# Mamba mixer in a vision tower: GpSimd makes the scan input of 4 of 16 units in SBUF, and the softplus scratch moves into an output buffer

## What is computed

```python
xz = einsum('bld,ed->ble', xn, in_proj_w)            # 512 -> 2 x 1024
x_inner, z = split(xz, 2)
xc = silu(causal_conv4(x_inner) + conv_b)            # 1024 channels
x_ssm = einsum('bld,ed->ble', xc, x_proj_w)          # 33 rows: B (16), C (16), one step
dt = softplus(x_ssm[..., -1:] * dt_w[:, 0] + dt_b)
A = -exp(A_log)                                      # 1024 x 16
def step(h, (dt_t, B_t, C_t, u_t)):
    h = exp(dt_t[..., None] * A) * h + (dt_t * u_t)[..., None] * B_t[:, None, :]
    y_t = sum(h * C_t[:, None, :], axis=-1) + D_param * u_t
return einsum('ble,de->bld', y * silu(z), out_proj_w) + residual
```

## Time and profile before

| what | value |
|---|---|
| median of 3 runs | 3200.05 us (3198.8 to 3203.89) |
| the profiled execution, its own time | 3196.83 us |
| its span in the profile | 3195.2 us |
| busy, whole span | PE 2581.1 us, DVE 1982.7, ACT 1351.8, POOL 1149.4 |
| mixer, first to last of its parts | about 455 us to 1721 us of the span |

### The profile page before, as it was taken

The page is one execution under the profiler, slowest core; times in us unless marked ns, Lnnn a source line. Parts: engine busy times, 40 slices in busy tenths (PEclk is TensorE's granted clock), DMA queues, the critical chain, the costliest instruction groups (busy, mean ns, idle before and its releaser), DMA issues. The chain is left out here.

```text
span 3195.2 us, 47773 instructions
## 1 busy us (share of the span) xinstructions
PE 2581.1 (81%) x17110; PEld 2128.3 (67%) x17111; DVE 1982.7 (62%) x2707; ACT 1351.8 (42%) x3260; POOL 1149.4 (36%) x694
## 2 busy tenths in 40 slices
PE   5999986778888888888877603999994699999997
PEld 5999986777788878788766501444442466666665
DVE  7557336999999999999995520222222655655453
ACT  1332527777777777777772200111110122222222
POOL 3000004666666666666662054010012422222110
PEclk9989978899988999999998756999997788988897
DMA  5600001000000000000000054555555110110000
GB/s 216 275 1 1 1 1 48 34 28 29 28 29 28 29 29 28 29 28 28 28 28 7 0 179 123 184 178 189 167 168 154 55 28 29 29 29 28 8 8 14
DMA packets 63510, 201.48 MB, mean 63 GB/s; under 512 B 12347, under 2 KB 17595, under 8 KB 60475
## 3 DMA queue, kind: packets, MB, share of 16 engines
q1 hardware_dynamic: 25210, 96.31, 8.9%
q0 software_dynamic: 26272, 80.77, 7.9%
q10 hardware_dynamic: 11808, 21.50, 1.8%
HBM read 130.31 MB, written 68.23 MB: 62 GB/s over the span
## 5 line engine op out<-in xcount | busy, mean ns | idle before, releaser
L832 POOL TENSOR_TENSOR m_hs<-m_hs,m_BC 128x1040 f32<-128x1040 f32 x256 | 617.0, 2410 | 333.5 <-DVE m_hs L940 333.5
L752 ACT ACTIVATE m_dA<-m_dt,m_A 128x128 f32<-128x128 f32 x2048 | 616.3, 388 | 268.6 <-DVE m_hs L940 149.6
L631 PE MATMUL m_py<-m_hs,ident 128*128 128x130 f32 x4096 | 568.1, 297 | 166.8 <-POOL m_hs L832 166.6
L631 PEld LDWEIGHTS m_py<-m_hs,ident 128*128 128x128 f32 x4096 | 534.4, 210 | 186.2 <-POOL m_hs L832 183.8
L940 DVE TENSOR_TENSOR_SCAN m_hs<-m_dA,m_own 128x1040 f32<-128x1040 f32 x256 | 593.4, 2318 | 21.6 <-DVE m_own L929 15.9
L929 DVE TENSOR_TENSOR m_own<-m_BC,m_own 128x1040 f32<-128x1040 f32 x256 | 317.7, 1241 | 11.4 <-DVE m_hs L940 3.6
L583 PE MATMUL m_pw<-m_xg,m_w_in 128*128 128x130 f32 x2048 | 259.4, 285 | 47.3 <-DVE m_xc L893 36.2
L583 PEld LDWEIGHTS m_pw<-m_xg,m_w_in 128*128 128x128 f32 x2048 | 249.1, 199 | 53.1 <-DVE m_xc L893 41.7
L1335 PE MATMUL e_pG<-e_w_gu,e_xT 128*128 x656 | 235.5, 503 | 11.0 <-issue 8.3
L1315 POOL DMA_DIRECT2D e_x<-slots x80 | 43.0, 538 | 403.8 <-PE e_pX L1326 396.9
L1335 PEld LDWEIGHTS e_pG<-e_w_gu,e_xT 128*128 128x128 f32 x656 | 119.8, 192 | 91.6 <-issue 25.4
(11 more groups left out here) (263 smaller groups left out, 4630.9 us busy)
## 6 DMA issues: line engine op xcount, KB each, us to landing
m_BC<-xs SPq DMA_DIRECT2D x16, 2080.0 KB, 8.7
slots<-a_zero POOLq DMA_DIRECT2D x48, 512.0 KB, 39.0
e_w_gu<-in_gate_up_w SPq DMA_DIRECT2D x32, 768.0 KB
e_x<-slots POOLq DMA_DIRECT2D x82, 256.0 KB
slots<-e_y ACTq DMA_DIRECT2D x82, 256.0 KB, 2.2
e_w_d<-in_down_w SPq DMA_DIRECT2D x32, 256.0 KB
out_h<-t_ho SPq DMA_DIRECT2D x8, 520.0 KB, 3.3
a_AT<-in_A_cols SPq DMA_DIRECT2D x8, 512.0 KB, 7.3
```

Source lines behind the costliest of these rows:

```text
L631: mm = pe.matmul(py[k % 2][:, 0:MT], ident[:, :], hs[u % NB][:, n, :], start=False, stop=(half == 1 and n == HN - 1))
L752: act.activation(images(dA[u % NB][:, n, :])[:, :, 1:TOK], images(dt[b][:, k, :])[:, :, 1:TOK], ACT.Exp, scale=A[:, at:at + 1]).then_inc(d ...
L832: pool.tensor_tensor(hs[u % NB][:, :, :], hs[u % NB][:, :, :], BC[b][:, ST + half * HN:ST + (half + 1) * HN, :], ALU.mult).then_inc(prod_r ...
```

## The change

POOL makes the scan's input of units 3, 7, 11 and 15 of every step, in a new SBUF tile `pool_bu`, out of three instructions; it does so behind its products of units 0, 4, 8 and 13. DVE's scan of those four units reads `pool_bu` in SBUF instead of `own` in PSUM, and DVE makes the input of the other twelve. DVE still makes `du` of all eight tiles. The scratch `ex` is dropped: Abs and Exp write into `y` of the parity of the step whose softplus they make, and so wait until the output projection of the step two before has read it. The stage before clears its semaphores and adds a barrier of all engines, so that their numbers can be used again.

```diff
 def ssm_kernels(...):
+    used = []
         def sem(name):
-            return ctx.enter_context(nc.semaphore("a_" + name))
+            used.append(nc.alloc_semaphore(name="a_" + name))
+            return used[-1]
...
+    nc.clear_and_free_semaphores(used)
+    nc.all_engine_barrier()
...
+POOL_UNITS = {3: 0, 7: 4, 11: 8, 15: 13}
...
-        ex = sb("ex", [P, ET, MT])
+        pool_bu = sb("pool_bu", [P, HN, MT])
...
+        own_du, own_rows, own_bu = map(sem, ("own_du", "own_rows", "own_bu"))
+        BUS = NU - len(POOL_UNITS)
+        PB = len(POOL_UNITS)
+        def pool_units(u):
+            return sum(v <= u for v in POOL_UNITS)
+        def dve_units(u):
+            return u + 1 - pool_units(u)
...
-            def steps(q, b, first=False):
+            def steps(q, b, first=False, reused=True):
...
                 act.wait_ge(x_ready, (q + 1) * ET)
+                ex = y[b]
                 if not first:
                     act.wait_ge(dt_ready, q)
+                if reused:
+                    act.wait_ge(out_done, (q - 1) * 2)
                 act.activation(ex[:, :, :], dt[b][:, :, :], ACT.Abs).then_inc(ln_steps, 1)
...
-                            steps(g + 1, 1 - b)
+                            steps(g + 1, 1 - b, reused=not first)
...
-            steps(0, 0, first=True)
+            steps(0, 0, first=True, reused=False)
...
-                    pool.tensor_tensor(e1[:, :, :], ex[:, :, :], e1[:, :, :], ALU.subtract).then_inc(log_steps, 1)
+                    pool.tensor_tensor(e1[:, :, :], y[b][:, :, :], e1[:, :, :], ALU.subtract).then_inc(log_steps, 1)
...
+            def input_of(g, b, v):
+                k, half = divmod(v, 2)
+                n = g * PB + pool_units(v)
+                rows = BC[b][:, half * HN:(half + 1) * HN, :]
+                pool.tensor_tensor(pool_bu[:, HN - 1, :], dt[b][:, k, :], xc[b][:, k, :], ALU.mult).then_inc(own_du, 1)
+                pool.wait_ge(own_du, n)
+                pool.tensor_tensor(pool_bu[:, 0:HN - 1, :], rows[:, 0:HN - 1, :],
+                                   pool_bu[:, HN - 1, :].unsqueeze(1).broadcast_to([P, HN - 1, MT]), ALU.mult).then_inc(own_rows, 1)
+                pool.wait_ge(own_rows, n)
+                pool.tensor_tensor(pool_bu[:, HN - 1, :], pool_bu[:, HN - 1, :], rows[:, HN - 1, :], ALU.mult).then_inc(own_bu, 1)
...
             def turn(g, b, last=False, more=True):     # POOL
                 pool.wait_ge(BC_in, (g + 1) * 16)
+                pool.wait_ge(u_ready, g + 1)
...
+                    for v, at in POOL_UNITS.items():
+                        if at == u:
+                            input_of(g, b, v)
                     if not last and LOG_AT <= u < LOG_AT + 4:
                         log_step(g + 1, 1 - b, u - LOG_AT)
...
-                    dve.wait_ge(du_ready, g * ET + k + 1)
-                    if u > 0 or not first:
-                        dve.wait_ge(scanned, g * NU + u)
-                    dve.tensor_tensor(bu..., BC[b]..., du[k % 3]..., ALU.mult).then_inc(bu_ready, 1)
+                    if u not in POOL_UNITS:
+                        dve.wait_ge(du_ready, g * ET + k + 1)
+                        if u > 0 or not first:
+                            dve.wait_ge(scanned, g * NU + u - ((u - 1) % NU in POOL_UNITS))
+                        dve.tensor_tensor(bu..., BC[b]..., du[k % 3]..., ALU.mult).then_inc(bu_ready, 1)
...
-                    dve.wait_ge(bu_ready, g * NU + u + 1)
+                    if u in POOL_UNITS:
+                        dve.wait_ge(own_bu, g * PB + pool_units(u))
+                    else:
+                        dve.wait_ge(bu_ready, g * BUS + dve_units(u))
...
+                    source = pool_bu[:, :, :].rearrange("p n t -> p (n t)") if u in POOL_UNITS else bu
                     dve.tensor_tensor_scan(hs[u % NB]..., dA[u % NB]..., source, 0.0, ALU.mult, ALU.add).then_inc(scanned, 1)
```

More of the change, by code:

```diff
@@ L925, in turn @@
                         dve.wait_ge(BC_in, (g + 1) * 16)
-                    dve.wait_ge(du_ready, g * ET + k + 1)
-                    if u > 0 or not first:
-                        dve.wait_ge(scanned, g * NU + u)
-                    dve.tensor_tensor(bu.rearrange("p (n t) -> p n t", t=MT), BC[b][:, half * HN:(half + 1) * HN, :],
-                                      du[k % 3].unsqueeze(1).broadcast_to([P, HN, MT]), ALU.mult).then_inc(bu_ready, 1)
+                    if u not in POOL_UNITS:
+                        dve.wait_ge(du_ready, g * ET + k + 1)
+                        if u > 0 or not first:
+                            dve.wait_ge(scanned, g * NU + u - ((u - 1) % NU in POOL_UNITS))
+                        dve.tensor_tensor(bu.rearrange("p (n t) -> p n t", t=MT), BC[b][:, half * HN:(half + 1) * HN, :],
+                                          du[k % 3].unsqueeze(1).broadcast_to([P, HN, MT]), ALU.mult).then_inc(bu_ready, 1)
                     if half == 0:
@@ L939, in turn @@
                         dve.wait_ge(summed, g * NU + u - NB + 1)
+                    source = pool_bu[:, :, :].rearrange("p n t -> p (n t)") if u in POOL_UNITS else bu
                     dve.tensor_tensor_scan(hs[u % NB][:, :, :].rearrange("p n t -> p (n t)"),
-                                           dA[u % NB][:, :, :].rearrange("p n t -> p (n t)"), bu, 0.0,
+                                           dA[u % NB][:, :, :].rearrange("p n t -> p (n t)"), source, 0.0,
                                            ALU.mult, ALU.add).then_inc(scanned, 1)
```

## The result

The changed kernel takes 3375.24 us in the median of 4 runs (3372.03 to 3383.18), the kernel before 3199.43 us: ratio 1.0556, 95% interval 1.0527 to 1.0585. The forecast was 3390 us, range 3325 to 3430. The profiled execution took 3378.41 us.

A forecast was written before the change was run, and what follows sets the result against it. The prediction took a step's loop through the engines, not DVE alone, as the bound. 94.7 + 39.8 + 34.5 + 14.3 + 5 + 4 + 1 = 193 us on the profiled 3196.8 us gave 3390 us, range 3325 to 3430.

The forecast's parts named there:

- The loop: A 76.0 us step runs dt_ready, scan 5, take_xs, Abs, dt_ready with hardly any slack; anything put in lengthens it.
- The scratch: Abs, now writing into the output buffer, waits for PE's second output part in 14 steps: +94.7 us.
- The rival of slowed output tiles: PE's part one runs at the lower clock, so Abs waits longer: 3430 to 3470 us, chance 0.08.
- One sign: In the profile after, POOL's idle time before the first log step grows from 91.5 us by nearly 95.
- POOL's three instructions: POOL's making of one scan input takes 2.9 us, bounds 2.7 to 3.4.
- Unit 15: Behind dt_ready, scan 15 waits for POOL's input and the residual step: 2.65 us in 15 steps, +39.8 us.
- The held `du`: DVE's du of the next step's units 0 and 2 is held by POOL's products: 15 times 2.3, +34.5 us.
- The race of scan and product: POOL's product, 0.03 us ahead, holds the scan reading pool_bu; unit 3 loses 0.95 us a step, +14.3 us.
- the sign that the prediction had named for its rival: If DVE wins the race: pool_bu scans of 2.3 us and products of 4.7; 3346 us, chance 0.33.
- scan 5 to `take_xs`, unit 7: Unit 7's scan loses 0.35 us or 0, because ACT leads take_xs: +5 us or 0.
- the last step behind scan 15: The last step has no softplus; its four scans cost +4 us or give back about 3.
- The semaphores: In the stage before, a clear and one more barrier, once: 1 us, bounds 0 and 5.

The follow-up runs named there:

- e_scratch: Changed kernel with no unit given to POOL: scratch stays in the output buffer, DVE makes all 16 inputs; ratio 1.0319, median 3294.43 us.
- e_11only: Changed kernel with only unit 11 given to POOL and the softplus scratch in tiles free at that time; ratio 1.0009.
- c_step: Kernel of c_log with ACT's softplus one unit earlier, behind dA of unit 11 instead of 12; ratio 0.9888, median 3162.31 us.
- c_log: Kernel before the change with POOL's four log steps set closer, behind the products of units 9, 10 and 11; ratio 0.9992.
- e_no15: Changed kernel with POOL making units 3, 7 and 11 only, DVE making the input of unit 15; ratio 1.0364, median 3312.74 us.
- e_pool: Changed kernel with its four POOL units, but the softplus scratch in tiles free at that time; ratio 1.0281, median 3285.01 us.
- e_work: e_pool, but DVE makes all 16 inputs and scans read PSUM; POOL still makes its four, unread; ratio 1.0104, median 3227.64 us.
- e_gate: Changed kernel with POOL's product ahead of each POOL unit waiting until that unit's scan is done; ratio 1.0426, median 3333.48 us.

## Why the prediction was right, by its steps

**The loop** was right, and the whole forecast hangs on it: e_scratch (a wait goes in one for one), e_11only (work off DVE in the slack part changes nothing) and c_step (a chain moved forward pays) show it from three sides. c_log shows where it ends: once `dt_ready` came 2.2 us earlier, the sum of unit 11 held DVE instead, and the step stayed as long.

**The scratch:** 94.7 us forecast, Abs waited 95.3. Alone it cost 89.8. That PE can't be earlier held: part one took 5.53 to 6.73 us, where it was 5.53 to 6.46 before. The rival of slowed output tiles did not come. One sign was off: POOL's idle time before the first log step grew by 73 us (91.5 to 164.3), not by nearly 95. In e_scratch it grew by 89.5; the prediction had left out that POOL's input for unit 11 stands in that idle time (e_11only: 69.3 us for 91.5).

**POOL's three instructions:** 0.46 + 1.94 + 0.46 us with two gaps of 0.08, 3.0 us in all for the 2.9 forecast. The short ones cost more than by the element (0.46 for 0.3), the long one less (2.13 ns an element for 2.3). The Trainium skill's figure (GPSIMD Engine Reference, Performance versus the Vector engine), an estimate of 2.5 us, was half a microsecond too low here.

**Unit 15:** `dt_ready` to the end of scan 15 was 6.15 us and is 1291.75 - 1283.04 = 8.7: 2.56 us a step for 2.65. e_no15 takes it out together with the next term.

**The held `du`:** this term was mis-sized, and it makes nearly all of the difference. I had 2.2 us for that of unit 0 and 0.1 for unit 2, in 15 steps. From the end of scan 0 to that of scan 1 it is 1301.27 - 1295.57 = 5.70 us for 3.89, so 1.8, and unit 2's is not held:

```profile
1293.25 2.32 DVE L981 TENSOR_TENSOR_SCAN m_hs<-m_dA,m_own 128x1040 f32<-128x1040 f32 x1
1295.49 2.10 DVE L937 TENSOR_TENSOR m_own<-m_dt,m_xc 128x130 f32<-128x130 f32 x1
...
1298.95 2.32 DVE L981 TENSOR_TENSOR_SCAN m_hs<-m_dA,m_own 128x1040 f32<-128x1040 f32 x1 [0.22 <-DVE m_own L966]
```

It is held in 14 steps, since the last step has no residual step ahead of it, for 26.5 us in all. And the step grows by less than that. From the end of scan 15 to that of scan 1 the 14 steps take 20.6 us more, to that of scan 2 only 18.7, for the 34.5 forecast. About half of what is missing from 26.5 is idle time that five steps already had at this place before the change, and that the hold now covers. The kernel before, at the first input of such a step:

```profile
1348.45 1.25 DVE L929 TENSOR_TENSOR m_own<-m_BC,m_own 128x1040 f32<-128x1040 f32 x1 [0.88 <-DVE m_hs L940]
```

This idle time was 0.85 to 1.05 us, and is 0.05 to 0.35 in the changed kernel: 3.8 us in all. `BC` had landed 25 us before it; the five steps are those with which the second to the sixth pass of the loop in the code begin. Why DVE stands idle there is open.

**The race of scan and product:** POOL won in all 16 scans of unit 3 and in 13 of the 16 of unit 7 (4.51 to 4.55 us). DVE won the other three, in unit 7 of the first step and of the two before the last: scans of 2.32 us and products of 4.52, the sign that the prediction had named for its rival. All of unit 11's scans but the last step's met no product and took 2.3 us. The size was 0.78 us for unit 3 (4.65 for 3.87) where I had 0.95. The Trainium skill's rule (SBUF — State Buffer, Who interferes with whom) is that issue order decides and the loser stands still. The trace agrees on the loser, with scans of 4.55 us behind POOL and products of 4.40 and 4.52 behind a scan. On the order it bears the rule out only where the lead is clear: with 0.07 us or more ahead POOL won every time, but at the lead of 0.02 to 0.03 us on which I had put all cases it won 24 of 27. The three that it lost show the same lead, and they are the same three in e_pool and in e_no15. So the choice of POOL as the winner was right in the main, but the 0.03 us didn't decide it; what did is not shown.

**Where 15 us were too many.** The mixer grew by 177.4 us, not 192. Cut at `dt_ready`, at the ends of scans, at `take_xs` and at Abs, the two traces give the growth by place:

| place | forecast, us | measured, us |
|---|---|---|
| Abs waits, 14 steps | 94.7 | 95.3 |
| `dt_ready` to the end of scan 15, 15 steps | 39.8 | 39.9 |
| scan 15 to scan 2, the held `du`, 14 steps | 34.5 | 18.7 |
| scan 2 to scan 3, 14 steps, and the first step whole | 14.3 | 12.4 |
| scan 5 to `take_xs`, unit 7, 14 steps | 5 | 3.1 |
| the last step behind scan 15 | 4 | 6.9 |
| the rest | 0 | 1.1 |

So the `du` term is 16 us too large, the two small terms of the race are 2 us too large each, and the last step is 3 us too small: all four of its scans lost the race there and took 4.5 us each. The first `dt_ready` to the second is 70.34 us for 69.75. That this step grew by 0.6 us only is no surprise: neither a late unit 15 nor a held `du` comes ahead of it, and of the 1.3 us that unit 3 costs it, 0.7 come back before Abs.

**The semaphores:** from the last ACT instruction of the stage before to POOL's first of the mixer it is 0.9 us for 0.3, 0.6 us for the 1 forecast. e_11only has the change of semaphores too and is as fast as the kernel before.

**What was not foreseen** is e_work. My theory put the cost of POOL's units at the scans alone; with the scans out of it 32 us stayed, most of them in `du`. The forecast knew of the held `du`, the expectation of the experiment forgot it; and the part that a busy POOL alone costs, unit 2's `du`, stood in the forecast with 0.1 us a step, where e_work shows 1.2.

## What to carry to other kernels

Before work is moved from a busy engine to an idle one, follow one step as a loop from wait to wait: the busiest engine's total was not the bound, and 16 inputs off it gave nothing while a softplus issued one unit earlier, on top of the closer log steps, gave 1%. A moved operand changes place too: a scan that reads PSUM ran through POOL's work, the same scan from SBUF waited for it, and one extra wait that kept the two apart was a gain. And a buffer that is reused to make room brings its last reader's time with it; ask when that reader is done, not whether the buffer is large enough.

## What the runs showed of the hardware

- DVE's scan with both inputs in SBUF takes the same 2.32 us as with one in PSUM when POOL is idle (2317 and 2320 ns in the median). Against a POOL product that started 0.02 us ahead (1239.15 and 1239.17, unit 7) it takes 4.54 us, in e_gate's order 2.32 again. At that lead the scan was held 24 times of 27; in the other three the product was, for 4.52 us.
- The hold goes both ways and by whole instructions: 4.40 us for a 2.40 us product behind a scan.
- A POOL instruction that is next in its own queue came ahead of a DVE instruction that waited for the semaphore of the POOL instruction before it: in all 14 steps that have a residual step it came ahead of scan 15 (which took 3.13 to 3.31 us), and in the last two steps the product did (4.48 us).
- POOL's `tensor_tensor` over 130 elements takes 0.45 to 0.54 us, over 910 with one operand repeated 1.94, over 1040 with two full ones 2.40.
